# Graph network coupling layer: waits for landed gathers between two runs of five on GpSimd, and copies of a step moved ahead on ScalarE

## The reference

```
R = relu(abs_distances[:, None] @ w1 + b1) @ w2 + b2        # 64 hidden, 384 weights for each edge
Y = spherical_harmonics(rel_vec)
Fj = features[src]                                          # the gather: 32 numbers for each edge
...
acc = acc + _NORM[i] * jnp.einsum('euv,ef,evi,ofi->euo', Rb[..., k], Yf, Fb, C)
...
out = out.at[dst].add(msg)
```

## Time and profile before

| | us |
|---|---|
| median of 3 runs, without the profiler | 20091.59 |
| lowest and highest of the three | 20086.42, 20103.31 |
| span of the profiled execution | 25995.0 |
| coupling stage in it | 13870 to 21700 |
| busy in the profiled execution: VectorE, GpSimd, TensorE, ScalarE | 16714.1, 13429.9, 9853.2, 6288.5 |

### The profile page before, as it was taken

One profiled execution on the slowest core, in us unless ns is written; L12 is line 12 of the kernel. 1 busy time (PEld: TensorE's weight loads), 2 busy tenths in 40 slices (PEclk: granted clock), 3 DMA queues, 4 the chain that ended last, 5 costly groups with the idle time before them and its releaser, 6 DMA issues.

```text
span 25995.0 us, 290953 instructions
## 1 busy us (share of the span) xinstructions
PE 9853.2 (38%) x63545; PEld 7350.7 (28%) x63546; DVE 16714.1 (64%) x23622; ACT 6288.5 (24%) x13799; POOL 13429.9 (52%) x14067
## 2 busy tenths in 40 slices
PE   0131000000000006765225666666666666324422
PEld 0131000000000006664223444444444444313421
DVE  9898574547344438888555666666666677555555
ACT  0002121112111105543002333333333345201400
POOL 0187676667777760000664555555555552363165
PEclk6555555555555559985556777777777776555555
DMA  1133434441000001116222000000000006424623
GB/s 14 25 33 27 29 31 29 29 29 13 6 6 6 6 15 48 41 52 227 69 69 18 9 10 9 9 9 9 9 9 9 9 10 144 137 64 87 205 65 61
DMA packets 1751558, 1095.98 MB, mean 42 GB/s; under 512 B 1217323, under 2 KB 1658124, under 8 KB 1750028
## 3 DMA queue, kind: packets, MB, share of 16 engines
q0 software_dynamic: 454272, 412.11, 13.3%
q1 hardware_dynamic: 1089532, 417.46, 6.8%
q10 hardware_dynamic: 207632, 265.14, 3.3%
HBM read 700.94 MB, written 391.12 MB: 42 GB/s over the span
## 4 chain that ended last, share of the span: by engine, by line
DVE 31%; another core or an unknown queue 21%; issue 17%; DVEq 12%; PE 11%; ACT 4%; DMA 2%; ACTq 1%; POOL 0%; SPq 0%; POOLq 0%
PE banks L1423 5%; DVE arena L1768 5%; DVE arena L1767 4%; DVE red L2523 4%; DVEq L2201 3%; DVE hot L2196 2%; DVE arena L1740 2%; DVE arena L2207 2%; DVE srcs L2516 2%; PE banks L1365 2%; PE banks L1410 2%; DVEq L498 1%; DVE arena L1585 1%; DVEq L2261 1%
## 5 line engine op out<-in xcount | busy, mean ns | idle before, releaser
L804 POOL DMA_INDIRECT srcs<-spread,nbx x2808 | 2653.2, 945 | 5691.9 <-issue 3372.8
L782 POOL DMA_INDIRECT gat<-tab,nbr x3328 | 3455.0, 1038 | 2537.8 <-issue 1271.9
L1423 PE MATMUL banks<-w2rows,dsts 128*128 128x384 f32 x6656 | 3443.8, 660 | 1030.2 <-DVE srcs L2516 699.0
L782 POOL DMA_INDIRECT gat<-tab,pay x3328 | 3161.6, 950 | 1077.4 <-issue 892.0
L748 POOL DMA_INDIRECT pay<-records,nbr x2560 | 2746.2, 1073 | 843.1 <-issue 827.1
L1208 PE MATMUL banks<-ident,arena 128*128 128x128 f32 x2240 | 436.2, 379 | 7154.4 <-DVE arena L1768 2837.8
L909 ACT COPY banks<-arena 128x1024 f32<-128x1024 f32 (+1 forms) x1508 | 1318.6, 875 | 6430.8 <-issue 2701.9
L2511 DVE TENSOR_TENSOR srcs<-banks,g_s 128x512 f32<-128x512 f32 x1664 | 1146.1, 689 | 2252.6 <-remote 1505.1
L1208 PEld LDWEIGHTS banks<-ident,arena 128*128 128x128 f32 x2240 | 400.7, 204 | 7190.5 <-DVE arena L1768 2844.2
L2523 DVE TENSOR_REDUCE red<-srcs 128x160 f32<-128x2560 f32 x832 | 2346.2, 2820 | 75.6
L1279 PE MATMUL banks<-srcs,hot 128*128 128x96 bf16 (+1 forms) x11232 | 1169.8, 281 | 3175.7 <-DVE hot L2196 2136.8
(11 more groups left out here) (392 smaller groups left out, 22029.8 us busy)
## 6 DMA issues: line engine op xcount, KB each, us to landing
spread<-srcs SPq DMA_DIRECT2D x936, 192.0 KB, 2.9
dsts<-key_rows SPq DMA_DIRECT2D x234, 512.0 KB, 4.1
spread<-srcs ACTq DMA_DIRECT2D x468, 204.0 KB, 2.4
staged<-gat SPq DMA_DIRECT2D x416, 148.0 KB
gat<-staged ACTq DMA_DIRECT2D x416, 148.0 KB, 2.1
dsts<-key_rows ACTq DMA_DIRECT2D x117, 512.0 KB, 4.3
gat<-tab,nbr POOLq DMA_INDIRECT x3328
gat<-tab,pay POOLq DMA_INDIRECT x3328
```

The source lines that it names most:

```text
L782: pool.indirect_dma_start(out=gatv(s, GC[pas])[:, t, :], out_offset=None, in_=TAB[pas], in_offset=bass.IndirectOffsetOnAxis(ap=row, axis=0 ...
L804: pool.indirect_dma_start(out=chunk_rows(s, c)[:, q, :], out_offset=None, in_=rows, in_offset=bass.IndirectOffsetOnAxis(ap=nbx[:, r, s * X ...
L1423: last = t_.matmul(bank[1 + 2 * (p % 2) + h][:, 0:384], hid_rows[:, s % 2, 2 * p + h, :], w2rows[:, :], start=True, stop=True)
```

## The change

On GpSimd the ten gathers of a step are dealt into two runs of five: one late gather and four of `gat`. Behind each run there is a new wait until the `gat` gathers of this step so far have landed (64 and then 128 counts of the step's `gat_in`). The geometry is split: the two products stand behind the first wait, the difference behind the second. On ScalarE the copies of `rx`, `fT`, `g_v` and `g_s`, with their waits for `msg_ready` and `gat_in`, now stand ahead of the copy of `dT` (with its wait for `dT_raw`) and of `weight_parts` (with its wait for `pay_in`).

```diff
@@ GpSimd, late_record @@
-            def late_records(i, s, first):
-                pool.wait_ge(nbr_in[s], nbr_count(1, EARLY_ITERS + i))
-                if not first:
-                    pool.wait_ge(rec_out[s], i * 16 + 16 * EARLY_ITERS)
-                pool.nop(nofuse=True)
-                for t in range(LATE_TILES):
-                    pool.indirect_dma_start(
...
+            def late_record(i, s, t, first):
+                if t == 0:
+                    pool.wait_ge(nbr_in[s], nbr_count(1, EARLY_ITERS + i))
+                    if not first:
+                        pool.wait_ge(rec_out[s], i * 16 + 16 * EARLY_ITERS)
+                    pool.nop(nofuse=True)
+                pool.indirect_dma_start(
...
@@ GpSimd, step of radial_gather @@
-                    if gathers:
-                        gather_step(PASS_L2, i + (s + 2) // SLOTS, s2, False, range(0, TPS // 2))
-                    if geo:
-                        for stage in range(2):
-                            geometry(n + 1, s1, stage)
-                    if gathers:
-                        gather_step(PASS_L2, i + (s + 2) // SLOTS, s2, False, range(TPS // 2, TPS))
-                    if with_late:
-                        late_records(i, s, first_late)
+                    for half in range(2):
+                        if with_late:
+                            late_record(i, s, half, first_late)
+                        if gathers:
+                            i2 = i + (s + 2) // SLOTS
+                            gather_step(PASS_L2, i2, s2, False, range(half * TPS // 2, (half + 1) * TPS // 2))
+                            pool.wait_ge(gat_in[PASS_L2][s2], i2 * (16 * TPS) + (half + 1) * (16 * TPS // 2))
+                        if geo:
+                            geometry(n + 1, s1, half)
@@ ScalarE, radial_round @@
                 wins = None if first else group_windows(act, ACT_ENGINE, win_dst, n - 2)
-                act.wait_ge(dT_raw, n + 1)
-                s_.copy(dT[:, :], bank[7][0:9 * TPS, 0:P // 2].bitcast(BF16)).then_inc(dT_ready, 1)
-                if not final:
-                    weight_parts(i + (s + 1) // SLOTS, (s + 1) % SLOTS)
                 if not first:
                     act.wait_ge(msg_ready, n + (STEPS - 1))
                 act.wait_ge(gat_in[PASS_L2][s], gat_count(PASS_L2, i))
...
                 s_.copy(g_s[:, b, :, 0:8], fv[:, :, 0:8]).then_inc(geo_ready, 1)
+                act.wait_ge(dT_raw, n + 1)
+                s_.copy(dT[:, :], bank[7][0:9 * TPS, 0:P // 2].bitcast(BF16)).then_inc(dT_ready, 1)
+                if not final:
+                    weight_parts(i + (s + 1) // SLOTS, (s + 1) % SLOTS)
```

More of the change, by code:

```diff
@@ L755, in collect @@
                     step(i, False)
-            def late_records(i, s, first):
-                pool.wait_ge(nbr_in[s], nbr_count(1, EARLY_ITERS + i))
-                if not first:
-                    pool.wait_ge(rec_out[s], i * 16 + 16 * EARLY_ITERS)
-                pool.nop(nofuse=True)
-                for t in range(LATE_TILES):
-                    pool.indirect_dma_start(
-                        out=late[:, s, t, :], out_offset=None, in_=records,
-                        in_offset=bass.IndirectOffsetOnAxis(ap=nbr[:, s, t:t + 1], axis=0),
-                    ).then_inc(rec_in[s], 16)
+            def late_record(i, s, t, first):
[5 more added lines that the diff above has]
+                pool.indirect_dma_start(
+                    out=late[:, s, t, :], out_offset=None, in_=records,
+                    in_offset=bass.IndirectOffsetOnAxis(ap=nbr[:, s, t:t + 1], axis=0),
+                ).then_inc(rec_in[s], 16)
             def gather_step(pas, i, s, first, tiles=range(TPS)):
```

## The result

The changed kernel takes 21404.49 us (median of 4 runs, 21402.14 to 21409.79) against 20089.0 us (20077.45 to 20103.31) for the kernel before on the same chip. The ratio is 1.0657, with a 95% interval of 1.0644 to 1.067: it is slower by 1315 us. I had predicted slower, but by 845 us, and the time lies above my range, which ended at 21200.

A forecast was written before the change was run, and what follows sets the result against it. Without the profiler, VectorE's 13.7 us a coupling step was taken as the bound, GpSimd's chain close at 13.3; 2.6 us of pauses made it 15.9. Over 384 steps, 20092 + 845 = 20937, say 20940 us; range 19,900 to 21,200.

The forecast's parts named there:

- rival A: Coupling stage: GpSimd's landing pauses take the step over, losing 0.3 to 3.0 us a step, 20,200 to 21,240 us; chance 0.70.
- GpSimd's 14.1 us by the rows: Coupling step on GpSimd before the change: ten gathers at 1.25 us plus 1.9 us from first product to next gather.
- The landing wait: GpSimd's new standstill behind each run of five gathers: 1.3 us a run, 2.6 a step, bounds 2.0 to 3.0.
- The account: Sorting, coupling and chunk stages: late TensorE results explain 5.2 of the profiled execution's 5.9 ms excess, leaving 0.7 ms.
- p = 13.3: GpSimd's timed coupling step without pauses, range 12.0 to 14.1; step goes from 13.7 to 15.9 us, 845 us over 384 steps.
- late releases: TensorE's results reaching waiting engines late while GpSimd gathers, in all stages; taken as the profiler's cost, absent from timed runs.
- VectorE's own bound of 13.7: Coupling step on VectorE when TensorE isn't late: 13.7 us, taken as the step's time before the change.
- The other 32 steps: Coupling steps with eight gathers: 13.4 us on GpSimd with pauses, under VectorE's 13.7, so no loss.
- The order of the gathers, the split of the geometry, ScalarE's copies: Coupling stage, GpSimd's and ScalarE's reordered work: each claimed to add nothing to the timed run.
- What the profile was to show: Coupling stage after: GpSimd pauses about 1.3 us, `fT` wait mostly gone, weight waits shorter, profiled step 16.7 to 18 us.
- B: Coupling stage: timed gathers take 0.95 us or less, so VectorE's 13.7 us hides the pauses; 20,090 us; chance 0.13.
- C: TensorE's `r_ready`, coupling stage: late releases are real and pauses let them through; 400 to 870 us gain; chance 0.17.

The follow-up runs named there:

- experiment 4: Changed kernel without its two new waits for landed gathers, keeping the runs of five, split geometry and earlier copies: 20071.78 us, ratio 0.9998 to the kernel before.
- experiment 7: Eighth `gat` gather of every coupling step left out: on the kernel before 20080.3 us, on the changed kernel 20880.66 us.
- experiment 8: All coupling-stage gathers of `gat` read one same row: on the changed kernel 23334.62 us, on the kernel before 20079.38 us.
- experiments 2 to 4: On the kernel before: ScalarE's part alone, ratio 0.9996; GpSimd's part alone, 1.0623 and again 1.0643; whole change without its two waits, 0.9998.
- experiment 5: Changed kernel without the first of its two waits, the one ahead of the geometry's products: 20642.46 us, ratio 1.028 to the kernel before.
- experiment 6: Changed kernel with the late gather behind each run's four `gat` gathers instead of ahead, both waits kept: 20402.61 us, ratio 1.0162 to the kernel before.
- experiment 1: Kernel before, unedited, profiled again: 20063.89 us, ratio 0.9996; profiled span 20053.4 us instead of 25995, coupling step 14.16 us.

## Why the prediction was wrong

The direction and the mechanism held: rival A, the pause added to GpSimd's chain, is what happens. The size didn't. By the steps of the prediction:

**GpSimd's 14.1 us by the rows: right.** The undisturbed profile has the same 1.25 and 1.9 us and a step of 14.16.

**The landing wait, 1.3 us a run: mis-sized, the largest term.** The pause is 1.62 and 1.79 us in the step shown. Over the stage the pauses sum to 1490 us; some 107 belong to 13 padding steps with two of 4.1, and the rest is 1383 / 401 = 3.45 us a step, where I had 2.6 and at most 2.96. The missing 0.85 us x 384 is 326 us. The landing itself was nearly right: the last count comes 1.43 us behind the last gather's end where I had 1.3, and within my bound of 1.48. What I put at nothing was GpSimd's own share. I had taken SyncE's instructions off the 1.48 us of the earlier trace rows, but GpSimd has waits and an empty instruction of its own behind the landing, and these bring the products 0.30 us and the difference 0.21 us after the last count: 0.51 us of the missing 0.85. Another 0.26 is 1.43 for 1.3, twice, and the rest is the runs that land later than the median. So the 1.48 us was no upper bound for a pause of GpSimd, only for a landing. The Trainium skill ("DMA: Bandwidth & Descriptors", anatomy of one DMA on the SWDGE path) has about 2.0 us fixed for one DMA. The trace has more, 2.36 us from the gather's start to its last count in the chain shown, and 0.94 + 1.62 to 1.79 = 2.6 to 2.7 us to GpSimd's next instruction. Its other rule, to issue early and wait late, the runs bear out: without the waits the same order costs nothing (experiment 4), with them 1315 us.

**The account and p = 13.3: a wrong step.** I took the late releases for the profiler's own cost. They weren't in the timed runs, that was right, but they are no cost of profiling either: that execution was disturbed as a whole, and none of the 13 other profiles kept, of before, after and the experiments, is longer than its kernel's timed runs by more than 0.2%. The account explained 5.2 of 5.9 ms, and I read the 0.7 ms left over as a sign that timed gathers are shorter than profiled ones. Nothing tied the remainder to GpSimd. Set against the undisturbed profile, the disturbed one is 3510 us longer ahead of the coupling stage (it starts at 13870 and at 10360 us), 1935 in it and 497 behind it, where the account had 2364, 2239 and 574: what the account missed lay ahead of the stage that I used it for, and in that stage it had 304 us too much. The rows said 14.1, and in the new order, with one gap fewer, it is 13.86 (experiment 4; I hadn't seen that gain). My 13.3 was 0.56 us short, 215 us in 384 steps. What disturbed the execution stays open, since it didn't come again.

**VectorE's own bound of 13.7: low as the bound of a step, which hid half of that.** It is right for VectorE alone and for a step in which TensorE is in time, and the earlier trace rows show such a step. But experiment 7 has a third of the steps at 14.8 to 15.3 us for want of TensorE's weights, with no GpSimd in the way, and puts the two engines together at 14.2; before's step is 14.16. I took one step for the mean. I so put the step before 0.46 us too low, and with it the loss 0.46 x 384 = 177 us too high: two errors that nearly cancel.

**The other 32 steps, nothing: wrong, some 83 us.** Of these, about 18 have eight gathers from many rows and go from 14.16 to 14.89 us, 13 us in all. The last 13 are padding, with pauses of 4.1 us, and go from 14.16 to 19.9, some 70 us (experiment 8). The trace of before couldn't show this, as nothing on GpSimd waited for a landing.

**The order of the gathers, the split of the geometry, ScalarE's copies: nothing, and right** (experiments 2 to 4).

The sum with what was measured: 384 steps x (17.39 - 14.16) = 1240 us, and 13 + 70 for the others, 1323 against 1315 measured. My own sum with these corrections is 845 + 326 + 215 - 177 + 83 = 1292 us. A second sum, by waits alone, is the pauses less the slack that experiment 4 shows: 1490 - 193 = 1297 us in after; 725 - (193 - 12) = 544 in experiment 5, where 562 were measured; 492 - 193 = 299 in experiment 6, where 322 were. All three come out within 25 us.

**What the profile was to show.** The pauses before the products and the difference are there, the wait for `fT` is gone, and VectorE's waits for weights are short. "The profiled coupling stage comes out shorter, at 16.7 to 18 us a step" reads as if confirmed, with 7215 / 416 = 17.3 against the earlier trace rows. It is a hit by luck: against an undisturbed profile of before the stage is longer by 1320 us, and the weights weren't late in before either. My reason there, that two pauses let TensorE's results through, is wrong.

**The rivals.** B, hidden, falls with p = 14.1. C falls with experiment 1: the timed step before is 14.16 us, not over 16.7. Its 0.17 also pulled my range down to 19,900, where the open cost was a pause bounded by another engine's wait. With pauses up to 1.8 us the upper end would have been 20,092 + 384 x (14.1 + 3.6 - 13.7) = 21,630.

## What to carry to other kernels

If a profiled execution is far longer than the timed ones, take another before arguing from its waits, and don't use what is left of an account of it to correct durations that its rows show plainly. A wait for the landing of what an engine has just issued costs the full landing on that engine's chain, and with it the engine's own waits and register work behind the landing, which used to be hidden; put other work of the same engine between issue and wait (the late gather alone gave back 993 of 1315 us), or let the waiting stand with the consumer a step later, as the kernel before does for nothing. When an added wait makes a latency visible for the first time, bound it by the same transfer with all its index patterns, the padding too, and add what the waiting engine still has to do before its next instruction.

## What the runs showed of the hardware

A gather by 128 indices holds GpSimd for 0.94 us; its last count comes 1.43 us after that, and GpSimd's next instruction 1.6 to 1.8 us after it, the same with one pause a step as with two (724.5 and 728.0 us in 414 waits). If its indices are all one row, the pause is 4.1 us, and the DMA engines are busy 0.27 of the stretch rather than 0.08, at fewer bytes. I had expected landing not to depend on the indices.

One execution of a kernel can be 25995 us long with late releases throughout, where 10 others of it lie between 20053.06 and 20073.86.

TensorE idles more in after's coupling stage, and its granted clock there is 0.76 of full speed on average, against 0.86 in before's; both are a mix of its two levels, 2.4 and 1.2 GHz. The same 20345 matmul instructions, but for one, are busy 5008 us instead of 4605. It isn't the cause of the loss: VectorE's wait for weights is 151.7 us in after and 178.7 in before.
